# A cross-attention kernel whose row-major copy of h is transposed on VectorE in 32 by 32 blocks instead of on TensorE

## The reference, cut to what matters

```python
# x: (4, 512, 1024), ctx: (4, 64, 1024), all float32; SCALING = 0.5
logits = einsum('bsh,nh->bsn', x, router_W) + router_b         # 8 experts
w      = softmax(logits)
a_sum  = einsum('bsh,arh->bsr', x, lora_A)                     # lora_A is the context tensor
upd    = einsum('bsn,bsnh->bsh', w, einsum('bsr,nhr->bsnh', a_sum, lora_B))
h      = nan_to_num(x + SCALING * upd, nan=0, posinf=1e4, neginf=-1e4)
Q, K, V = h @ Wq.T + bq, ctx @ Wk.T + bk, ctx @ Wv.T + bv      # 32 heads of 32
attn   = softmax(where(mask, Q K^T / sqrt(32), -inf))
z      = h + (attn @ V) @ Wo.T + bo                            # h is needed a second time, as residual
out    = (z - mean(z)) / sqrt(var(z) + 1e-5) * ln_g + ln_b     # over the 1024 features
```

## Time and profile before

| | |
|---|---|
| median of 3 runs | 671.59 us (671.24 to 671.71) |
| the profiled execution | 671.83 us |
| its span, first to last instruction | 669.9 us |
| mean granted TensorE clock in the span | 0.996 |
| busy share of the span: PE, PEld, DVE, ACT, POOL | 98%, 85%, 72%, 45%, 31% |
| first phase (to the first scores matmul) | to 335.4 us of the span |

### The profile page before, as it was taken

One profiled execution on the slowest core, in us unless ns is written; L12 is line 12 of the kernel. 1 busy time (PEld: TensorE's weight loads), 2 busy tenths in 40 slices (PEclk: granted clock), 3 DMA queues, 4 the chain that ended last, 5 costly groups with the idle time before them and its releaser, 6 DMA issues.

```text
span 669.9 us, 10841 instructions
## 1 busy us (share of the span) xinstructions
PE 658.7 (98%) x3687; PEld 571.9 (85%) x3687; DVE 480.9 (72%) x917; ACT 298.4 (45%) x903; POOL 205.2 (31%) x215
## 2 busy tenths in 40 slices
PE   8999999999999999999999999999999999999995
PEld 7988879888988889888888989888888898898884
DVE  5778894578547774577566687888888888888634
ACT  5462262112231032311156676666766766666511
POOL 0110001100020002000433343656656566566653
PEclk9999999999999999999999999999999999999998
DMA  8946692435683357711665993424434344513311
GB/s 303 389 132 194 173 331 104 160 95 191 217 296 115 93 210 261 272 58 49 237 189 214 377 363 81 143 91 161 109 101 169 99 165 116 159 64 112 125 64 64
DMA packets 86503, 114.67 MB, mean 171 GB/s; under 512 B 23728, under 2 KB 59184, under 8 KB 86448
## 3 DMA queue, kind: packets, MB, share of 16 engines
q1 hardware_dynamic: 86256, 113.72, 50.4%
q10 hardware_dynamic: 192, 0.26, 0.1%
HBM read 67.81 MB, written 46.14 MB: 170 GB/s over the span
## 4 chain that ended last, share of the span: by engine, by line
PE 94%; DVE 2%; DMA 1%; ACT 1%; SPq 1%; issue 0%; DVEq 0%; ACTq 0%
PE ps L587 27%; PE ps L589 27%; PE ps L588 27%; PE ps L649 4%; PE ps L744 4%; PE ps L681 2%; PE ps L661 1%; DMA ctx_t<-ctxT 1%; PE ps L620 1%; PE ps L621 1%; PE ps L623 1%; SPq L381 0%; DVE w_lo L817 0%; DVE z_sb L1026 0%; DVE q_sb L919 0%
## 5 line engine op out<-in xcount | busy, mean ns | idle before, releaser
L587 PE MATMUL ps<-wo_hi,cx_hi 128*128 128x512 f32 x256 | 104.5, 408 | 0.0
L1146 ACT ACTIVATE s_sb<-s_sb,s_min 128x64 f32<-128x64 f32 x256 | 86.2, 338 | 36.9 <-DVE s_min L945 36.9
L587 PE MATMUL ps<-act_hi,w_hi 128*128 128x512 f32 x256 | 101.4, 396 | 0.3 <-DVE kv_sb L827 0.3
L589 PE MATMUL ps<-wo_hi,cx_lo 128*128 128x512 f32 x256 | 100.3, 392 | 0.0
L588 PE MATMUL ps<-wo_lo,cx_hi 128*128 128x512 f32 x256 | 100.2, 391 | 0.0
L589 PE MATMUL ps<-act_hi,w_lo 128*128 128x512 f32 x256 | 99.9, 390 | 0.0
L588 PE MATMUL ps<-act_lo,w_hi 128*128 128x512 f32 x256 | 99.9, 390 | 0.0
L1210 POOL TENSOR_TENSOR u_sb<-a_sb,w_sb 128x512 f32<-128x512 f32 x16 | 18.6, 1183 | 247.1 <-DVE w_sb L861 241.1
L1111 ACT ACTIVATE act_hi<-h_t 128x512 fp32r<-128x512 f32 x32 | 20.2, 633 | 156.9 <-DVE h_t L909 156.9
L1228 POOL TENSOR_TENSOR s_sb<-s_sb,s_min 128x256 f32<-128x256 f32 x64 | 39.4, 616 | 134.6 <-DVE s_min L945 134.6
L940 DVE SCALAR_TENSOR_TENSOR s_sb<-ps,mask_f 128x512 f32<-128x512 f32 x64 | 44.2, 691 | 46.4 <-PE ps L589 44.8
(11 more groups left out here) (118 smaller groups left out, 1528.1 us busy)
## 6 DMA issues: line engine op xcount, KB each, us to landing
q_cols<-q_sb SPq DMA_DIRECT2D x32, 512.0 KB, 3.3
qb<-q_cols SPq DMA_DIRECT2D x64, 256.0 KB, 3.7
x_sb<-xT SPq DMA_DIRECT2D x32, 256.0 KB, 3.1
h_rows<-hn_sb SPq DMA_DIRECT2D x32, 256.0 KB, 3.1
output_weights<-wo_sb SPq DMA_DIRECT2D x32, 256.0 KB, 3.0
z_sb<-h_rows SPq DMA_DIRECT2D x16, 512.0 KB, 4.3
out<-z_sb SPq DMA_DIRECT2D x15, 512.0 KB, 2.8
stage<-WvT SPq DMA_DIRECT2D x8, 512.0 KB, 5.0
```

The costliest lines, as they stand in the source:

```text
L587: pe.matmul(dst, lh, rh, start=(first and j == 0), stop=False)
L589: mm = pe.matmul(dst, ll, rh, start=False, stop=(last and j == n - 1))
L1146: act.activation(s_sb[c % 4][:, h, :], s_sb[c % 4][:, h, :], ACT.Exp, bias=s_min[c % 2][:, h:h + 1], scale=-1.0, accum_out=s_sum[c % 2][:, ...
```

## The change

The transposes leave TensorE. VectorE transposes `h_t` in blocks of 32 by 32 straight from SBUF to SBUF, and the blocks are stored in DRAM as they lie. So that a block belongs to 32 neighbouring features, the host reorders the features of x, the context and the weights (`by_blocks`). The bias `bo`, now one value a partition, is added on ScalarE, in place in `h_t`, after `act_lo` has been made. Two chunks share one store of 512 KB. A tile of 128 tokens is loaded by four DMAs of 32 partitions, in pieces of 256 bytes.

```diff
     def up(i, c, between=(), ahead=()):
-        return ([("rows", i, c - 2), ("copy", i, c - 2)] if c >= 2 else []) + [*ahead, ("update", i, c), *between, ("select", i, c)]
+        return ([("rows", i, c - 2)] if c >= 2 else []) + [*ahead, ("update", i, c), *between, ("select", i, c)]
...
-        beside[i] = {n: rows(i, 5 + n) if n in (1, 2) else [] for n in range(KC)}
+        beside[i] = {n: [("flush", i, 5 + n)] if n in (1, 2) else [] for n in range(KC)}
...
-    h_d = nc.dram_tensor("h_rows", (NB, TOK, H), F32, kind="Internal").ap()
+    h_d = nc.dram_tensor("h_rows", (NB, P // B, KC // 2, B, BLOCKS, 2 * B), F32, kind="Internal").ap()
...
-        hn_sb = [at(f"hn_sb{k}", [P, TT, P], AT_HN + 2048 * k) for k in range(2)]
+        hn_sb = [at(f"hn_sb{k}", [P, BLOCKS, 2, B], AT_HN + 4096 * k) for k in range(2)]
...
@@ SP
-            def bias_in():
-                sp.dma_start(bo_b[:], bo.unsqueeze(0).to_broadcast([P, H])).then_inc(bo_in, 16)
+            def mask_load():
...
-            def store_h(m):
-                sp.wait_ge(hn_copied, m + 1)
-                sp.dma_start(h_cols[m // KC, m % KC], hn_sb[m % 2][:]).then_inc(hn_stored[m % 2], 16)
-
-            def update(i, c):
-                if c >= 2:
-                    store_h(KC * i + c - 2)
+            def rows(i, c):
+
+                if c % 2:
+                    sp.wait_ge(hn_copied, KC * i + c + 1)
+                    j = (KC * i + c) // 2
+                    sp.dma_start(h_pieces[i, c // 2], hn_sb[j % 2][:].rearrange("p t k n -> p (t k n)")).then_inc(hn_stored[j % 2], 16)
...
-                sp.dma_start(z_sb[n % 4][:], h_tiles[n]).then_inc(res_in[n % 4], 16)
+
+                for t in range(P // B):
+                    sp.dma_start(z_sb[n % 4][B * t:B * t + B].rearrange("p (m n) -> p m n", n=2 * B),
+                                 h_tokens[n // TT, n % TT * (P // B) + t]).then_inc(res_in[n % 4], 16)
...
@@ PE
-            def h_rows(i, c):
-                m = KC * i + c
-                pe.wait_ge(h_ready, m + 1)
-                wait(pe, hn_copied, m)
-                for t in range(TT):
-                    mm = pe.transpose(ps_hn[:, t * P:(t + 1) * P], h_t[m % 3][:, t * P:(t + 1) * P], ident[:])
-                mm.then_inc(hn_mm, 1)
...
@@ DVE
-            def copy_h_rows(m):
-                c = m % KC
-                if m == 0:
-                    dve.wait_ge(bo_in, 16)
-                dve.wait_ge(hn_mm, m + 1)
-                wait(dve, hn_stored[m % 2], 16 * (m // 2))
-                dve.tensor_tensor(hn_sb[m % 2][:], ps_hn.rearrange("p (t n) -> p t n", t=TT),
-                                  bo_b[:, c * P:(c + 1) * P].unsqueeze(1).to_broadcast([P, TT, P]), ALU.add).then_inc(hn_copied, 1)
...
+            def rows(i, c):
+                m = KC * i + c
+                j = m // 2
+                dve.wait_ge(h_shifted, m + 1)
+                wait(dve, hn_stored[j % 2], 16 * (j // 2))
+                dve.transpose(hn_sb[j % 2][:, :, m % 2, :], h_t[m % 3][:].rearrange("p (t n) -> p t n", n=B)).then_inc(hn_copied, 1)
...
             def flush(i, c):
-                copy_h_rows(KC * i + c)
+                rows(i, c)
                 if c == KC - 2:
                     h_low(KC * i + KC - 1)
...
@@ ACT
+            def add_bias(m):
+
+                act.wait_ge(hlo_done, m + 1)
+                act.activation(h_t[m % 3][:], h_t[m % 3][:], ACT.Identity, bias=bo_c[:, m % KC:m % KC + 1]).then_inc(h_shifted, 1)
+
+            def flush(i, c):
+                if c == KC - 2:
+                    add_bias(KC * i + KC - 1)
+
             def select(i, c):
                 m = KC * i + c
+                if c:
+                    add_bias(m - 1)
                 act.wait_ge(h_ready, m + 1)
...
@@ host
+    def by_blocks(a):
+
+        a = np.asarray(a)
+        return a.reshape(*a.shape[:-1], P // B, KC, B).swapaxes(-3, -2).reshape(a.shape)
...
-        "xT": lay(x, 0, 2, 1),
+        "xT": lay(by_blocks(x), 0, 2, 1),
```

More of the change, by code:

```diff
@@ L28 @@
 LOG = R + NR
+B = 32
+BLOCKS = TOK // B
 SCALE = float(HD) ** -0.5
@@ L60 @@
 AT_HN = AT_H_T + 6144
-AT_QS = AT_HN + 4096
+AT_QS = AT_HN + 8192
 AT_STAGE = AT_QS + 8192
 AT_A_RHS = AT_STAGE + 16384
-AT_BO = AT_A_RHS + 2304
-AT_WO_SB = AT_BO + 4096
+AT_WO_SB = AT_A_RHS + 2304
 Q_FIRST = (0, 1, 5, 4, 6, 7, 2, 3)
@@ L105, in first_phase @@
     out += [("route", 0), ("keys", 5)] + split("B", 2, 3) + [("keys", 6), ("expand", 0, 0)] + split("V", 0)
-    out += [("keys", 7), ("keys_out",), ("expand", 0, 1)] + split("V", 1) + [("values", 0)] + split("V", 2) + [("bias_in",)]
+    out += [("keys", 7), ("keys_out",), ("expand", 0, 1)] + split("V", 1) + [("values", 0)] + split("V", 2) + [("mask_in",)]
     for c in range(KC - 1):
@@ L109, in first_phase @@
     out += up(0, 7, split("Q", 5, 4), [("values_out",)])
-    beside = {0: {1: rows(0, 6) + split("Q", 6) + [("key_parts", 0)], 2: rows(0, 7) + split("Q", 7) + [("key_parts", 1)],
+    beside = {0: {1: [("flush", 0, 6)] + split("Q", 6) + [("key_parts", 0)], 2: [("flush", 0, 7)] + split("Q", 7) + [("key_parts", 1)],
                   3: split("Q", 2) + [("mask",), ("key_parts", 2)], 4: split("Q", 3) + [("key_parts", 3)], 5: [("route", 1)]}}
     for i in range(1, NB):
-        beside[i] = {n: rows(i, 5 + n) if n in (1, 2) else [] for n in range(KC)}
+        beside[i] = {n: [("flush", i, 5 + n)] if n in (1, 2) else [] for n in range(KC)}
         if i < NB - 1:
@@ L151, in second_phase @@
     left = {s: [("query", last, 0, s + 2)] for s in range(6)}
-    left[0] += [("rows", last, KC - 1), ("flush", last, KC - 1)]
+    left[0] += [("flush", last, KC - 1)]
     left[4] += [("exit_high", last, 0, 0)]
@@ L188, in output_group, with xattn_kernel @@
     return (4 * (p - 1), c % 2) if c >= 6 else (4 * (p - 2) + 1 + c // 2, c % 2)
-def xattn_kernel(nc, xT, ctxT, mask, BT, rW, rb, WqT, WkT, WvT, bqkv, WoT, bo, ln_g, ln_b, out):
+def xattn_kernel(nc, xT, ctxT, mask, BT, rW, rb, WqT, WkT, WvT, biases, WoT, ln_g, ln_b, out):
     x_v = xT.rearrange("b (k p) t -> b k p t", p=P)
@@ L218, in xattn_kernel @@
         ident = sb("ident", [P, P])
-        bias_c = sb("bias_c", [P, 3, KC])
-        bq_c, bk_c, bv_c = (bias_c[:, k, :] for k in range(3))
+        bias_c = sb("bias_c", [P, 4, KC])
+        bq_c, bk_c, bv_c, bo_c = (bias_c[:, k, :] for k in range(4))
         rw_c = sb("rw_c", [P, KC, NR])
@@ L551, in step @@
                     for k in range(2):
[L552 removed]
+                        sp.wait_ge(hn_stored[k], 16 * ALL // 4)
                 if s == 15:
@@ L574, in step @@
                         (load_res if load else store_out)(n)
-            run({"half": half, "split": split, "key_parts": key_parts, "values_out": values_out, "bias_in": bias_in, "update": update, "select": select,
+            run({"half": half, "split": split, "key_parts": key_parts, "values_out": values_out, "mask_in": mask_load, "rows": rows, "select": select,
                  "flush": flush, "exit_low": exit_low, "pair_out": pair_out, "output_weight_in": output_weight_in,
@@ L655, in expand @@
                     pe.wait_ge(u_ready, TT * i + t + 1)
-                    if t == 1:
-                        wait(pe, hn_copied, KC * i)
                     if t >= 2:
@@ L787, in _ @@
             run({"keys": keys, "values": values, "route": a_and_logits, "expand": expand, "update": update,
-                 "rows": h_rows, "query": query, "pair": pair, "step": step})
+                 "query": query, "pair": pair, "step": step})
         @block.vector
@@ L901, in select @@
                 dve.wait_ge(bound_ready, m + 1)
-                wait(dve, hn_mm, m - 2)
+                wait(dve, hn_copied, m - 2)
                 wait(dve, hhi_done, m - 2)
@@ L1016, in _ @@
             run({"context_in": context_in, "adapter": adapter, "half": half, "split": split, "key_parts": key_parts,
-                 "values_out": values_out, "mask": mask_addend, "route": router, "expand": expand, "copy": copy, "update": update,
+                 "values_out": values_out, "mask": mask_addend, "route": router, "expand": expand, "rows": rows, "update": update,
                  "select": select, "flush": flush, "exit_low": exit_low, "pair_out": pair_out, "output_weight": output_weight,
@@ L1194, in _ @@
                  "values_out": values_out, "route": router_exp,
-                 "expand": expand, "select": select, "exit_high": exit_high, "pair_out": pair_out,
+                 "expand": expand, "select": select, "flush": flush, "exit_high": exit_high, "pair_out": pair_out,
                  "output_weight": output_weight, "zero": zero, "step": step})
@@ L1268, in lay @@
         return np.ascontiguousarray(a.transpose(axes) if axes else a)
+    def by_blocks(a):
+        a = np.asarray(a)
+        return a.reshape(*a.shape[:-1], P // B, KC, B).swapaxes(-3, -2).reshape(a.shape)
     arrays = {
-        "xT": lay(x, 0, 2, 1),
-        "ctxT": lay(np.asarray(ctx_4096).reshape(NB * V, H), 1, 0),
```

(13 more changed lines are left out.)

20 lines of the change are left out of this document (6 added, 14 removed).

## The result

The changed kernel takes 697.93 us (four runs, 692.87 to 701.70), the kernel before it on the same chip 671.65: a ratio of 1.0386, 95% interval 1.0352 to 1.0421. It is slower by 26 us, where 12 us of gain were forecast. Its four times are two pairs, 692.87 and 695.13 us at a mean granted clock of 0.965 and 700.73 and 701.70 us at 0.955; the profiled execution, 700.73 us with a span of 698.9, is of the slower pair.

A forecast was written before the change was run, and what follows sets the result against it. PE was taken as the bound: 15.8 us from removed transposes, less 1.3 in batch 0 and 2.3 waiting for x, gives 12.2 us gained, so 659.5 us; forecast 657.5 to 662, range 655.5 to 665.

The forecast's parts named there:

- DMAs and SP: Stores of h, `bo` load, tile loads: nothing waits for the stores, so nothing gained; the four tile loads costed at zero.
- the landing of x: Last x chunk before `route` in batches 1 and 2: landing adds 2.7 us after its issue.
- rival (d): VectorE bounds the first phase if a transpose takes beyond about 1.75 us: slower, 679 us at 2.0; chance 0.06.
- Rival (c): Second phase: tile loads come late, PE loses about 1 us in each of 8 pairs, 667.5 us; chance 0.08.
- the Trainium skill's rule of 512 bytes: Tile loads in 256-byte pieces: transfers under 512 bytes miss line rate; by it, the late-tile-loads time of 667.5 us.
- The 1.24 us: VectorE's transpose of a chunk of four, estimated from the table's 311 ns per 128x128 in bf16.
- 32 x 0.49: PE's saving from dropping the transposes of 32 chunks, given as 15.8 us, the most this route can give.
- 10 places at 1.6 - 0.81: Batch 0's chunks and flush, batches 1 and 2's last x: a 1.6 us transpose exceeds VectorE's 0.81 us gap, losing 7.5.
- three more issues: Tile loads: extra issues of 0.4 to 0.9 us each, so all four are there after 4.3 to 8.4 us.
- PE's wait for `kv_sb`, start of batch 0's queries: Batch 0: VectorE becomes the bound and PE idles about 0.8 us there; about 0.4 us of gain lost.
- PE's wait for Q6's split: Batch 0 flush: ScalarE's bias for chunk 7 comes before splitting Q6, so PE waits 0.9 us.
- PE's waits for x at `route`: Batches 1 and 2: PE reaches the next x before it lands, waiting 1.4 and 0.8 to 0.9 us, 2.3 together.

The follow-up runs named there:

- experiment 4: Kernel before the change, last x chunk of batches 2 and 3 loaded by two DMAs of 122 and 6 partitions: 696.90 us, ratio 1.0371.
- experiment 1: Changed kernel with h's DRAM layout and feature order rearranged so that each store runs on 16 engines: 660.09 us, ratio 0.9832.
- experiment 8: Kernel before the change, each 256 KB store of h cut into DMAs of 124 and 4 partitions (4 engines): 687.29 us, ratio 1.0212; profiled at 680.07.
- experiment 11: The kernel of experiment 8 run again for its profile, nothing else changed: 688.22 us.
- experiments 2: Changed kernel, its DRAM layout kept, each store of h cut into four DMAs of 32 partitions (16 engines each): 664.81 us, ratio 0.9897.
- experiment 7: The kernel of experiment 1 with each store cut into DMAs of 104 and 24 partitions (13 and 12 engines): 664.21 us, ratio 0.9894.

## Why the prediction was wrong

**The step that failed** is "DMAs and SP": "Half as many stores of h, in long pieces, ...: nothing waits for them, so nothing is gained" stood for a cost of zero. Nobody waits for the store, that holds. But the step looked at who waits for the store, and not at who is behind it. I looked at the length of its pieces (4 KB, good) and at their number, not at the shape of the destination: 4 groups of 32 rows. That leaves it 4 engines and some 10.6 us, and a quarter of each load of x stands behind it on just these; the loads of `qb` and of the keys come late in the same way. The forecast had priced the landing of x at the 2.7 us of the earlier trace rows, a figure that holds only as long as nothing else is on the engines. It was 7.5 and 8.1.

**The second thing missing** was the price of a wait. Every wait of my sum counted once. Here a wait of TensorE of some 4 us costs its length and then 8 us more, as experiment 4 shows by itself (12.6 us for 4.2). Most of the loss is this: 26.8 of the 43.7 us.

**Rivals.** The slower rival (d) had the right sign and the wrong mechanism: the transpose took 0.70 us, not 1.75 or more. Rival (c), late loads because of small pieces, was about the wrong tensor: the tile loads land in 3.3 us each, and VectorE waits for none of them after the change. In experiment 1 the first tile's four took 8.2 us in all and VectorE waited 0.8 us there, where the prediction had allowed up to 1. What the Trainium skill's rule of 512 bytes, in "DMA: Bandwidth & Descriptors", "Specifications", costs these loads was thus covered; PE waited for none of it. The 1.24 us estimated from the Trainium skill's table, in "VectorE: DVE Perf Modes", "The three transpose paths", did not hold either: it is 0.698 us, as the nearest row suggested. Some of the working is off without deciding anything: 32 x 0.49 is 15.7, 10 places at 1.6 - 0.81 are 7.9 and not 7.5, and three more issues put the tile at 5.5 to 7.0 us, not 4.3 to 8.4.

**What held**, read from experiment 1, where the rest of the change stands alone:

| step | forecast | measured |
|---|---|---|
| time, from all terms | 659.5 us | 660.09 (659.68 in profile) |
| transpose of a chunk on VectorE | 0.69 | 0.70 |
| PE's wait for `kv_sb`, start of batch 0's queries | 0.8 | 0.9 |
| PE's wait for Q6's split | 0.9 | 0.8 |
| PE's waits for x at `route` | 1.4 and 0.85 | 0.9 and 0.5 |
| first scores matmul | about 323 us | 323.30 |
| from one chunk to the next, batch 2 (issues of x) | 5.44 | 5.44 |
| from the first scores matmul to the end | 334.5 | 334.6 |

The waits for x came out 0.85 us smaller together and the time 0.1 larger in the profile, so some other tenths are unaccounted for. The gain for the transposes was not measured by itself. The period of a chunk, 5.93 us in the kernel before and 5.44 now, bears out the 0.49 us of each.

**What stays open.** What length of wait lets the clock fall is not settled: those of 0.5 and 0.9 us in experiment 1 did not, one of 1.6 did in the changed kernel, one of 2.5 did not in experiment 8, one of 2.4 did in experiment 11 (at the same place), and all of 2.8 us or more did. Nor is it settled how long it stays low: 3.41 us behind the waits of 2.8 to 3.7 us before the first scores, 17.07 or 20.48 behind those of 4.1 us and more for x, but 17.07 behind the 1.6 and the 2.4 for x as well. The changed kernel's faster pair was not profiled; that it lacks batch 1's stretch fits its clock and its time and was not seen. Where the stretch of experiments 2 and 7 sits in their slower executions was not caught.

## What to carry to other kernels

Count, for every DMA that a change adds or reshapes, on how many engines it runs: look at the outermost dimension of both sides, and see whether dimensions that lie apart leave a small number there. Then check the count in the trace, by the updates of the DMA's semaphore: mine was wrong for 104 partitions. A store that nobody waits for still holds up what is issued behind it, from either of the two queues tried; in a profile the sign is that the landing time of its neighbours has grown, here from 3 to 6 us. A landing time that is missing on the page says only that the DMA has fewer than 16 engines: it is missing for the harmless store of experiment 7 too. And in a kernel that keeps TensorE full, price a wait of several microseconds at its length plus half a stretch of 17 us of low clock, not at its length.

## What was not expected of the hardware

- A DMA of 512 KB from 128 partitions took 4.0 us on 16 engines at the median and 10.6 on 4: 2.6 times as long, not 4.
- During the store on 4 engines the mean busy share of all 16 was 1 to 4 tenths at some 100 GB/s, and x, 256 KB, which landed in 2.7 us in the kernel before, took 8.2 when ScalarE's queue issued it.
- Of an x load behind that store, 12 of the 16 updates came after 2.5 to 3.2 us and the last four after 5.3 to 7.5 us (batch 2): a DMA is as late as the busiest of its engines.
- Stored by 104 and 24 partitions, the same 512 KB ran on 13 and 12 engines (25 late updates) and left x its 2.7 us.
- VectorE transposed 128x512 float32 in 32 by 32 blocks in 698 ns at the median, nearly the 686 ns of a two-input pass over as many elements.
- Waits of 4.1 and 4.3 us of TensorE each brought 17.07 us at a granted clock of 0.5, waits of 5.1 to 6.3 us 17.07 or 20.48.
